# Eight chunk buffers, and a DMA transposition of the attention rows, in an attention and feed-forward kernel

## The reference

```python
xn = layernorm(x)
q, k, v = (heads(xn @ W.T) for W in (Wq, Wk, Wv))
scores = where(causal, einsum('bhqd,bhkd->bhqk', q, k) / sqrt(32), min)
attn = merge_heads(einsum('bhqk,bhkd->bhqd', softmax(scores), v)) @ Wo.T
gate = silu((xn @ fp8(gate_w)) * gate_scale)
up = (xn @ fp8(up_w)) * up_scale
ffn = ((gate * up) @ fp8(down_w)) * down_scale
out = x + attn + ffn
```

## Time and profile before

| what | value |
|---|---|
| median of 3 runs | 1428.94 us (1428.7 to 1429.1) |
| profiled execution | 1425.56 us, span 1423.8 us |
| mean granted TensorE clock | 0.988 |
| PE busy | 1325.6 us, 93% |
| DVE busy | 1111.2 us, 78% |
| ACT busy | 945.0 us, 66% |
| POOL busy | 919.7 us, 65% |
| DMA queue of SP | 28.5% of 16 engines |

### The profile page before, as it was taken

How to read it: one execution, slowest core, us unless ns; L and a number is a source line. 1 busy time by engine, 2 the same in 40 slices (tenths; PEclk the granted TensorE clock), 3 DMA queues, 4 the chain that set the end, 5 groups by cost and what they waited for, 6 DMA issues and landing times.

```text
span 1423.8 us, 34052 instructions
## 1 busy us (share of the span) xinstructions
PE 1325.6 (93%) x12254; PEld 856.1 (60%) x12254; DVE 1111.2 (78%) x2982; ACT 945.0 (66%) x1790; POOL 919.7 (65%) x1171
## 2 busy tenths in 40 slices
PE   4878899988799999999999999999999999999987
PEld 2434444433566666666767676766767676766754
DVE  7868888887787887878787887878787887878763
ACT  3332222221788887888888787878888887878851
POOL 0100111110688888988888888888888888888862
PEclk9999999999899999999999999999999999999999
DMA  6454766624321211212121212212121212222121
GB/s 211 125 160 120 205 187 186 173 92 148 79 61 32 76 47 47 72 36 76 39 76 47 69 39 69 77 46 76 32 77 45 76 39 68 65 58 76 32 61 60
DMA packets 116410, 119.56 MB, mean 84 GB/s; under 512 B 27090, under 2 KB 84690, under 8 KB 116242
## 3 DMA queue, kind: packets, MB, share of 16 engines
q1 hardware_dynamic: 116242, 117.38, 28.5%
HBM read 74.86 MB, written 42.21 MB: 82 GB/s over the span
## 4 chain that ended last, share of the span: by engine, by line
PE 55%; DVE 11%; ACT 4%; issue 3%; POOL 1%; DMA 0%; SPq 0%; ACTq 0%; DVEq 0%
PE bank L1256 16%; PE bank L1270 12%; PE bank L1234 8%; PE bank L171 7%; PE bank L1221 7%; PE bank L1289 4%; DVE junk L194 2%; DVE probs L912 2%; ACT probs L1046 2%; DVE ga L1158 2%; DVE mx L199 1%; DVE fu L1163 1%; PE bank L1280 1%; ACT th L1053 1%; POOL probs L912 1%
## 5 line engine op out<-in xcount | busy, mean ns | idle before, releaser
L1076 ACT ACTIVATE p<-bank,s_exp 128x512 f32<-128x512 f32 x576 | 398.1, 691 | 184.3 <-PE bank L1221 179.5
L912 POOL TENSOR_TENSOR probs<-p,probs 128x512 f16<-128x512 f32 x448 | 519.8, 1171 | 0.0
L1046 ACT CAST probs<-p 128x512 f16<-128x512 f32 x576 | 353.9, 614 | 0.1
L1006 POOL TENSOR_SCALAR_AFFINE_SELECT p<-p 128x256 f32<-128x256 f32 (+1 forms) x320 | 152.2, 475 | 139.2 <-ACT p L1076 137.6
L171 PE MATMUL bank<-k_st,q_st 96*128 96x512 f16 (+3 forms) x792 | 221.8, 328 | 18.7 <-DVE mx L194 9.8
L199 DVE TENSOR_REDUCE mx<-bank 128x1 f32<-128x512 f32 x264 | 180.0, 685 | 65.6 <-PE bank L171 60.9
L1221 PE MATMUL bank<-q_st,k_st 98*128 98x512 f16 (+3 forms) x768 | 221.3, 329 | 7.5 <-DVE k_st L1166 5.7
L1234 PEld LDWEIGHTS bank<-v_sb,probs 128*128 128x128 f16 x4608 | 197.8, 97 | 50.2 <-issue 1.6
L1234 PE MATMUL bank<-v_sb,probs 128*128 128x65 f16 x4608 | 213.9, 192 | 2.6 <-DVE attn L1125 2.6
L1256 PE MATMUL bank<-xt,wg 128*128 128x256 f16 x1536 | 200.2, 273 | 5.2 <-DVE fu L1163 5.2
L1256 PE MATMUL bank<-xt,wu 128*128 128x256 f16 x1536 | 199.4, 273 | 0.0
(11 more groups left out here) (115 smaller groups left out, 1720.5 us busy)
## 6 DMA issues: line engine op xcount, KB each, us to landing
q_st<-q_parts SPq DMA_DIRECT2D x201, 64.0 KB, 2.0
k_st<-k_parts SPq DMA_DIRECT2D x201, 64.0 KB, 2.0
v_sb<-v_parts SPq DMA_DIRECT2D x66, 132.0 KB, 2.2
xt<-xn_parts SPq DMA_DIRECT2D x17, 512.0 KB, 4.5
v_parts<-v_st SPq DMA_DIRECT2D x8, 1056.0 KB, 7.5
x_in<-in_L_attn_x SPq DMA_DIRECT2D x8, 1024.0 KB, 6.3
xn_parts<-x_t SPq DMA_DIRECT2D x16, 512.0 KB, 7.8
q_parts<-qk_st SPq DMA_DIRECT2D x32, 256.0 KB, 4.1
```

The lines of the kernel that those rows point to most:

```text
L912: ops.tensor_tensor(probs[s % 2][:, LO, at], p32[k % RING][:, :], probs[s % 2][:, HI, at], ALU.subtract).then_inc(signal, 1)
L1006: nc.gpsimd.affine_select(out=at, in_=at, compare_op=ALU.is_ge, fill=0.0, base=0, pattern=[[0, blocks], [1, P]], channel_multiplier=-1).th ...
L1046: nc.scalar.copy(probs[s % 2][:, HI, u * 512:(u + 1) * 512], p32[k % RING][:, :]).then_inc(p_hi, 1)
L1076: nc.scalar.activation(p32[k % RING][:, :], st_bank[(s + u) % 2][:, :], ACT.Exp, scale=s_exp[:, :]).then_inc(exp_done, 1)
```

## The change

`qk_st` and its semaphores get eight buffers, one for each of the eight q and k chunks of a tile, and ACT's wait becomes one for the store of the same chunk of the tile before. `w_raw` gets three buffers in place of four; the fourth matrix is loaded into the first buffer after the first matrix is split. In the second stage the eight transposes on PE and the copy on ACT are replaced by one `dma_start_transpose` from `a_part` to `a_t`, issued by SP behind `store_row` of the heads s = 1 and 2. ACT waits for it before it writes `a_part` again, and PE before it projects. The four late pairs keep the transposes on PE, with a semaphore of their own, `late_turned`.

```diff
-TURN_STEP = {17: 0, 25: 1}
...
-        w_raw = [sb(f"w_raw{m}", [P, KC, D], F32) for m in range(4)]
+        w_raw = [sb(f"w_raw{m}", [P, KC, D], F32) for m in range(3)]
...
-        qk_st = [sb(f"qk_st{i}", [P, 2, TILE], F16) for i in range(4)]
+        qk_st = [sb(f"qk_st{i}", [P, 2, TILE], F16) for i in range(8)]
...
-            for m, w in enumerate(weights):
-                sp.dma_start(w_raw[m][:, :, :], w.rearrange("(c p) k -> p c k", p=P)).then_inc(w_loaded[m], 16)
+            def load_weights(m):
+                sp.dma_start(w_raw[m % 3][:, :, :], weights[m].rearrange("(c p) k -> p c k", p=P)
+                             ).then_inc(w_loaded[m], 16)
+
+            for m in range(3):
+                load_weights(m)
                 if m in (0, 2):
                     load_x(m // 2)
             load_ffn_weights(0)
...
+            sp.wait_ge(w_hi_done, 1)
+            sp.wait_ge(w_lo_done, 1)
+            load_weights(3)
...
-                        for i in range(4):
-
-                            sp.wait_ge(qk_stored[i], 16 * 2 * (S // TILE))
+                        for i in (0, KC):
+
+                            sp.wait_ge(qk_stored[i], 16 * (S // TILE))
...
-                        wait(act, qk_stored[c % 4], 16 * (2 * t + c // 4))
-                        nc.scalar.copy(qk_st[c % 4][:, HI, :], bank[2 + c % 4][:, :]).then_inc(hi_done, 1)
+                        wait(act, qk_stored[c], 16 * t)
+                        nc.scalar.copy(qk_st[c][:, HI, :], bank[2 + c % 4][:, :]).then_inc(hi_done, 1)
...
                     store_row(sp, rows, (s + 1) % 4, n + 2)
+                    if with_out and s in (1, 2):
+                        turn_attention(s - 1, it - LAG)
...
+            def turn_attention(i, r):
+                sp.wait_ge(split_done, 2 * r + i + 1)
+
+                wait(sp, op_mm, 2 * r + i)
+                sp.dma_start_transpose(a_t[:, :, :, :].rearrange("p w k t -> p (w k) t"),
+                                       a_part[:, :, :].rearrange("p w d -> p (w d)")).then_inc(turned, 16)
...
-                        if with_out and k - 1 in TURN_STEP:
-                            act.wait_ge(turn_mm, 2 * (it - LAG) + TURN_STEP[k - 1] + 1)
-                            nc.scalar.copy(a_t[:, :, :, :].rearrange("p w k t -> p (w k t)"),
-                                           misc[:, :].bitcast(F16)).then_inc(turned, 1)
...
                             act.wait_ge(o_done, 2 * HEADS_PER_IT * it)
+
+                            wait(act, turned, 16 * (2 * r + i))
                             nc.scalar.copy(a_part[:, HI, :], attention_rows(i, r)).then_inc(split_link, 1)
...
-                            if k in TURN_STEP:
-
-                                pe.wait_ge(mt_copied, 4 * it + 3 + TURN_STEP[k])
-                                turn_attention(TURN_STEP[k], r)
                             for i, piece in PROJ_STEP.get(k, ()):
+                                if piece == 0:
+
+                                    pe.wait_ge(mt_copied, 4 * it + 3 + i)
+                                    pe.wait_ge(turned, 16 * (2 * r + i + 1))
                                 project(i, piece, r)
```

More of the change, by code:

```diff
@@ L309, in prepare @@
         lo_done = sem("lo_done")
-        qk_stored = [sem(f"qk_stored{i}") for i in range(4)]
+        qk_stored = [sem(f"qk_stored{i}") for i in range(8)]
         v_stored = sem("v_stored")
@@ L403, in _ @@
             over_tiles(tile)
-            for i in range(4):
-                sp.wait_ge(qk_stored[i], 16 * 2 * NT)
+            for i in range(8):
+                sp.wait_ge(qk_stored[i], 16 * NT)
             sp.wait_ge(v_stored, 16 * NT)
@@ L552, in weights_max @@
                 dve.wait_ge(w_loaded[m], 16)
-                nc.vector.tensor_reduce(w_max[:, at], w_raw[m][:, :, :], AX.XY, ALU.max,
+                nc.vector.tensor_reduce(w_max[:, at], w_raw[m % 3][:, :, :], AX.XY, ALU.max,
                                         apply_absolute_value=True).then_inc(pow_link, 1)
@@ L694, in tile @@
                     if c < 8:
-                        nc.vector.tensor_tensor(qk_st[c % 4][:, LO, :], src, qk_st[c % 4][:, HI, :],
+                        nc.vector.tensor_tensor(qk_st[c][:, LO, :], src, qk_st[c][:, HI, :],
                                                 ALU.subtract).then_inc(lo_done, 1)
@@ L895, in attend @@
         turned = sem("turned")
+        late_turned = sem("late_turned")
         op_mm = sem("op_mm")
@@ L920, in attend, with late @@
                   for i in range(2)]
+        def late(i, r):
+            return 2 * (r - (NIT - LAG)) + i
         def attention_rows(i, r):
@@ L973, in _ @@
             sp.wait_ge(xt_loaded, 16 * (NIT + 1))
+            sp.wait_ge(turned, 16 * 2 * (NIT - LAG))
         @block.gpsimd
@@ L1106, in _ @@
                 for i in range(2):
-                    act.wait_ge(turn_mm, 2 * r + i - 1)
+                    wait(act, turn_mm, late(i, r) - 1)
                     nc.scalar.copy(late_part[i][:, HI, :], attention_rows(i, r)).then_inc(split_link, 1)
@@ L1129, in copy_turned @@
             def copy_turned(i, r):
-                dve.wait_ge(turn_mm, 2 * r + i + 1)
+                dve.wait_ge(turn_mm, late(i, r) + 1)
                 dve.wait_ge(op_mm, 2 * r + i - 1)
                 nc.vector.tensor_copy(late_t[i].rearrange("p w k t -> p (w k t)"),
-                                      bank[i][:, :].bitcast(F16)).then_inc(turned, 1)
+                                      bank[i][:, :].bitcast(F16)).then_inc(late_turned, 1)
             def add_output(i, r, src=misc):
@@ L1273, in down, with turn_attention @@
                     mm.then_inc(down_mm, 1)
-            def turn_attention(i, r, out=misc, src=a_part):
+            def turn_attention(i, r, out, src):
                 pe.wait_ge(split_done, 2 * r + i + 1)
@@ L1284, in project @@
             def project(i, piece, r, out=misc, src=a_t):
-                if piece == 0:
-                    pe.wait_ge(turned, 2 * r + i + 1)
                 products = [(ap, wp, kc) for ap, wp in TERMS for kc in range(KC)]
@@ L1360, in last_turn @@
             def last_turn(i, r):
-                pe.wait_ge(turned, 2 * r + i - 1)
+                wait(pe, late_turned, late(i, r) - 1)
                 turn_attention(i, r, bank[i], late_part[i])
@@ L1367, in last_project @@
                 pe.wait_ge(o_ready, 2 * r + i - 1)
+                pe.wait_ge(late_turned, late(i, r) + 1)
                 for piece in range(PROJ_PIECES):
```

6 lines of the change are left out of this document (3 added, 3 removed).

## The result

The changed kernel takes 1404.53 us (1403.87 to 1404.98, four runs) where the kernel before took 1429.02 (1428.7 to 1430.38, four runs) on the same chip: a ratio of 0.9825, with a 95% interval of 0.9809 to 0.9841. The forecast was 1406 in a range of 1401 to 1431.

What follows compares the result with a forecast made beforehand. TensorE was taken to bound the second stage's projecting iterations, with ScalarE's store waits delaying the first stage. From the 1428.9 us median, 11.0 (buffers), 10.8 (transposes) and 1 (ScalarE's copy) came off: 1406, range 1401 to 1431.

Steps and rivals of the forecast that it cites:

- rival C: First stage: the buffers bring nothing because the late stores turn into another wait; 1417 us, chance 0.03.
- Tiles 2 to 5: First stage: without ScalarE's store waits, TensorE's four waits for VectorE's chunk split go, 6.2 us in all.
- Tile 6: First stage: x_high starts once the normalised x is there, moving the chain through GpSimd's x_low to VectorE's rounding by 2.4 us.
- Tile 7: First stage, no next x: ScalarE's 3.62 us wait goes, VectorE is free 2.44 us earlier; worth 2.4.
- The clock at the 5.00 us idle: Tile 6, TensorE's wait for a row maximum: a shorter idle could spare 2.3 us of lower clock, counted only in the range.
- TensorE's groups: Second stage: removing transposes saves 0.45 us twice in each of 12 iterations, 10.8 us.
- Rival D: Second stage: TensorE gains nothing because VectorE, busy 159.50 of 200 us, sets the steps; 1418 us, chance 0.05.
- 1 us from ScalarE's copy: Second stage, second half: the exp starts 0.3 us sooner without the copy, up to 3.6 us, of which 1 taken.
- T, the transposition's time: Second stage, DMA issue to landing: taken as 4.5 us, hidden within rooms of 7.1 and 5.1 before the projection's halves.
- rival B: Second stage: transposition blocks go in series, fine-grained, T of 10.9 us, stalls of 115 us; 1521 us, chance 0.19.
- The turn at T = 7.0: Second stage: stalls of 1.9 us an iteration, 22.8 in 12, make the change slower than before from this landing time.
- Rival A: Second stage: T between 5.1 and 7.0, only the second half stalls; at 6 us 10.8 come back, 1417; chance 0.13.

Runs made afterwards that it cites:

- run 1: The eight q and k chunk buffers and three weight buffers alone, on the kernel before: 1413.9 us against 1425.8, ratio 0.9917.
- run 8: The changed kernel with VectorE's first rounding in tile 6 of the first stage moved behind chunk 5, not chunk 4: 1401.34 us against 1425.49, ratio 0.9829.
- run 3: The kernel before with only the three weight buffers and Wo's later load, four chunk buffers kept: 1425.6 us against 1425.36, ratio 1.0.
- Run 5: The changed kernel with TensorE still making the eight transposes at steps 17 and 25, results unused: 1414.89 us, periods of 64.32 to 64.34.
- run 4: The changed kernel with ScalarE still making an unread 128x1024 fp16 copy at steps 18 and 26: 1405.31 us against 1425.8.
- run 6: The changed kernel with two unread DMA transpositions of Wo issued ahead of each real one: 1424.53 us against 1425.36, ratio 0.9993.
- the repeated run: The changed kernel run again, unedited, against the kernel before on another chip: 1405.04 us against 1425.49, ratio 0.9855.
- run 7: The changed kernel with four unread DMA transpositions of Wo issued ahead of each real one: 1505.67 us against 1425.36, ratio 1.0562.

## Why the prediction was right, point by point

- **Chunk buffers, 11.0 us forecast, 11.1 in the traces and 11.9 in run 1's medians.** The mechanism stood: the waits for the stores went, and nobody else took them up (rival C fell in run 1). But the three terms were each off and their errors met, which is luck. The transposes of the next x by TensorE (L737, now L744), one group in each tile, mark the tiles. Before, the groups behind tiles 1, 5 and 6 start at 118.85, 264.35 and 308.86; after, at 118.61, 255.64 and 298.28.
  - Tiles 2 to 5, forecast 6.2: 145.50 - 137.03 = 8.5 us. TensorE's four waits for chunks were the 6.2; about 2 more came from the waits at the tile starts, "issue" 9.7 and then 7.6, which I had not counted. They shrank with the lateness.
  - Tile 6, forecast 2.4: 44.51 - 42.64 = 1.9. I let x_high start with the normalised x; in the changed kernel it starts at 277.50, behind the chunk cast of 277.02, which waits 2.17 us for TensorE.
  - Tile 7, forecast 2.4: (361.13 - 308.86) - (350.00 - 298.28) = 0.55. This trace is at the low end: over all eight profiles with the changed first stage the stretch is 51.1 us in the mean, over the three with the old one 52.4, so 1.3. The term failed in its step "VectorE is late from there to the stage's end". SP's rows show that the stage ends with the landing of the last store of v:

```profile
341.72 0.36 SPq L403 DMA_DIRECT2D v_parts<-v_st  x1
```

```profile
DMA to landing us min/median/max: 6.5/6.5/6.5
```

341.72 + 6.5 = 348.2, and the next stage's first DVE row follows at 349.03. Before, it was issued at 353.53 and took 5.8 us; in the seven other profiles with the changed first stage it took 5.5 to 6.1. So 0.7 us was lost in that landing in this trace, and VectorE, with its wait for the store gone, had one of 1.20 us for TensorE's chunk in its place.
- **The clock at the 5.00 us idle, put at the edge: right.** The changed kernel still has the spell at the lower clock in tile 6 (0.83 over 280 to 300 us). It is gone where the waits are broken up (1.00 in run 8).
- **Weight buffers, nothing: right** (run 3).
- **TensorE's groups, 0.45 us each, 10.8 us: right.** 12 x 0.88 = 10.6. Run 5 puts them back and the periods with them. Rival D fell: VectorE did not set the steps.
- **1 us from ScalarE's copy: wrong, it is nothing** (run 4). The exp does start about 0.2 us sooner without the copy, but nothing that sets the period waits for it. That VectorE's maxima pass it on, as I assumed, is the step that failed in this term.
- **T, the transposition's time, forecast 4.5, bounds 2.2 and far above: 3.2 us.** Choosing by the store of the same size, and not by the load in small pieces, was right; rival B's series of slow pieces does not show at this size. The Trainium skill's 1309 ns for a 128x128 block (VectorE: DVE Perf Modes, section The three transpose paths) would make it an estimated 10.5 us in series; the trace shows 3.2 for eight blocks, so that price is not paid once a block. In the queue each further one adds 1.3 us (run 6: 2.63 for two), that is 256 KB in 1.3 us or about 200 GB/s. The Trainium skill, DMA: Bandwidth & Descriptors, section Latency and other measured facts, has 261 GB/s; this run gives somewhat less, but the 1.3 us are the time that SP takes to issue one, and the rate of the transfers alone is not shown.
- **Rooms of 7.1 and 5.1 us: right to 0.1 us.**
- **The turn at T = 7.0: too late.** Run 6 has its landing at 6.0 us and is level with the kernel before. The step that failed is "each excess is paid 12 times" and no more: beyond the excess, 12 x 1.0 us, come 0.3 us at each wait before the first matmul (17.0 us in all), and spells at the lower clock. The margin of the change over no change is 6.0 - 3.2 = 2.8 us of landing, not 3.8. Rival A's 10.8 us at T = 6 was 19.5.
- **The total, 22.8 us off: right on this chip with some luck.** Measured are 24.5 here, and 20.5 both between the spans and on the chip of the repeated run (1425.49 - 1405.04). Against 20.5 the forecast is 2.3 too high: 1.0 for ScalarE's copy, 0.2 in TensorE's groups, and the late period of 1.06. The 24.5 come from the kernel before, which has 1429.0 on this chip and 1425.4 to 1425.8 on the three others; the changed kernel has 1404.5 and 1405.0.

## What to carry to other kernels

Price an engine's relief by the engine that is never idle in that stretch: 0.45 us groups on a TensorE that was busy 99% of the time came back whole, and 1.04 us copies on a ScalarE with idle of its own came back not at all. A DMA that replaces an engine's work needs its room measured from the place in the queue where it can be issued to the first reader, and that room wants a reserve, since missing it by 1 us cost 1.6 a period and missing it by more cost the clock too. When a stage's stall goes, look at what ends the stage; here it was the landing of one store. And before a gain is put down to an edit, lay the two traces side by side stage by stage: run 8 took 3.7 us off, but the 2.5 us between its trace and that of the unedited kernel lay at the other end of the program.

## What the runs showed of the hardware

- A DMA transposition of 128x1024 fp16 in SBUF: 3.1 to 4.8 us from issue to landing, 1.25 us on SP's queue, about 1.3 us for each further one behind it.
- A VectorE TENSOR_SCALAR on 128x768 in SBUF takes 0.56 us, and 4.31 when it starts 0.2 us behind a GpSimd TENSOR_TENSOR of 4.10 us (tiles 2 to 6 of the changed kernel); in run 8 another one, of 0.55 us, took 1.89. Both end 0.4 us after GpSimd's. A SCALAR_TENSOR_TENSOR on two SBUF tensors took 4.70 us in place of 0.96 in the same way (tile 0). A TENSOR_TENSOR that reads a bank (0.69) and a reduction (0.94) beside GpSimd's operation in run 8 kept their times.
- TensorE's clock behind a wait: after 3.97 us of idle (run 7) four matmuls of 128x512 kept 1.02 us and the next four took 1.90. All twelve waits of 3.75 us and more in that run had such a spell behind them; so had two of 1.92 and 2.08 us in run 6, while one of 2.83 us in run 7 had none. Behind one and the same wait of 3.33 us at the end of the program the granted clock over the next 5.3 us was 0.50, 0.68 or 1.00, by the trace. What decides stays open.
- One period in one of the profiles was 1.06 us longer through a late row of maxima; what held that DMA stays open.
